# Second gated network's fills cut into pieces and its successor's loads moved, with three stages' last norm and sum on VectorE

## The chip, the cores and the metric

The program runs on one core of one Trainium2 chip. Its engines are TensorE (PE, matmuls), VectorE (DVE), ScalarE (ACT), GpSimd (POOL) and SyncE (SP, which here only issues DMAs); each has an instruction stream of its own, and they wait for one another through semaphores. The metric is the device time of one execution in microseconds (us); lower is better.

## What is computed

The reference takes x of shape (8, 512, 256) in float32 and adds to it, four times, a layer-normed sublayer of the layer-normed x:

```python
x = x + _layernorm(_L0_attn_ref(_layernorm(x)))   # differential attention, 16 heads
x = x + _layernorm(_L0_ffn_ref(_layernorm(x)))    # 2 x (window attention, gated network), each with its own residual
x = x + _layernorm(_L1_attn_ref(_layernorm(x)))   # token diffusion (16 heads), then channel diffusion
x = x + _layernorm(_L1_ffn_ref(_layernorm(x)))    # 8 experts, the best 2 of each token
# the gated network, in _L0_ffn_ref's _layer:
h = shift_token(x)                                # half the channels one token later
h = (h - mu) / sqrt(var + 1e-05) * lg + lb
a, g = split(h @ w1 + b1)                         # 682 channels each
x = x + (a * gelu(g)) @ w2 + b2
```

`_layernorm` subtracts the mean of the 256 channels and divides by sqrt(variance + 1e-5).

## The kernel before, in words

The work is a chain of seven stages, built by `build`: differential attention (names a_), window attention and gated network of layer 0 (w_, f_), the same two of layer 1, diffusion attention (c_), and the mixture of experts (d_). Both layers' tiles carry the same names in the profile, so w_ and f_ stand for two stages each; the first gated network runs from about 1690 to 1948 us of the span, the second from about 2480 to 2775. A stage reads its input from DRAM and writes its output there, in 8 batches (b = 0 to 7) of 512 tokens. A batch is one tile [128 partitions, 4 token tiles, 256 channels], 1024 numbers a partition. At its end a stage closes with a barrier of all engines (`Stage.close`, L37 to L39).

A stage's neighbour is given to it as `following`. While a stage still works, it already does the next one's first steps: `ahead_sync` issues the next stage's first loads on SP, `ahead_fill` writes its constant tiles on POOL, `ahead_gpsimd` takes its first roots on POOL (in diffusion also the norm of its input), and `ahead_vector` takes its first statistics on DVE (in diffusion also the set-up of scales and of the doubled weight wqk). The last batch's result is written to a tile of the next stage, `handed`, so that it can be stored while that stage begins; `arrived` counts that store.

*The gated network* (`gated_ffn`, L1503 on) takes each batch as follows. SP loads the shifted input (`load`, L1571 to L1574) and the residual y_res; DVE takes its statistics (`take_stats`), POOL takes the inverse root (`roots_in.step`, L102 and L104: add eps, raise to -1/2), and DVE normalises (`norm_input`, four tensor_scalar, L112) into hn. PE transposes hn (L1699), ACT brings it back as hT, PE multiplies with w1 in six chunks (L1710, L1716), ACT takes the gelu, DVE the product (`multiply`, L1786), and PE multiplies with w2 into ps_y (L1735). The order on DVE is written out: after the product of chunk 0 the statistics of the batch before's output (second network only), after chunk 1 `take_stats` of the next batch, after chunk 3 `norm_input` of the next batch, after chunk 4 the bias added to y_res (L1816), and after all chunks the sum with ps_y (`add_output`), which gives `y_taken`. PE runs one chunk ahead of DVE's products by two PSUM buffers.

In the second network (`LAST`, layer 1) the output is also normed and added to x: DVE writes the sum to yn (L1795), and POOL does `norm_output` of batch b - 1 in batch b: the root, four tensor_scalar (L1668), then one tensor_tensor with x_res (L1673); SP stores it in the next turn of its loop (L1626) and then loads the next x_res (L1646). SP's loop stands in this order: load of batch b + 1, `clear` (first network only: 4128 KB of zeros for the experts' lists, L1634), the store of batch b - 1 (second network), the wait for `y_taken` of batch b, the store of batch b (first network), and y_res of b + 1.

Where the steps of the next stage stand before the change: `ahead_sync` behind SP's loop; `ahead_fill` on POOL in batch 5 (`b + 3 == B`), a memset of packed_qk's rows 64 to 95 for all 16 heads at once (L1983), one of ones (L1985), one of v (L1986) and two small ones; `ahead_vector` on DVE in batch 7 behind chunk 2; `ahead_gpsimd` on POOL behind its loop, followed by `norm_output` of batch 7. DVE's `take_stats` and `norm_input` of batch b + 1 wait for SP's load and POOL's root; memsets stand on POOL right behind that root.

*Differential attention* (`differential_attention`, L120 on) goes by 16 steps a batch; the tail of batch b - 1 is spread over the steps of batch b, and for the last batch over a `drain` in which nothing else runs. In it: step 10 and 11 the output's statistics on DVE, step 11 POOL's root, step 12 DVE's norm (y) and POOL's `add_residual` (L393, x_res += y), step 14 DVE's `sum_stats` and POOL's root, step 15 POOL's `norm_sum` (L386), which SP stores (`store_normed`, L326) as the input of window attention.

*Diffusion attention* (`diffusion_attention`, L1831 on) ends its last batch in `drain` too: DVE's last statistics (L2682, L2687), POOL's root (L102, L104), POOL's four tensor_scalar (L2184) and its sum (L2189) into the experts' `handed`; the stage's barrier follows.

## Time and profile before

| | us |
|---|---|
| median of 3 runs | 4137.27 (4133.03 to 4146.78) |
| the profiled execution, its own time | 4133.88 |
| its span | 4132.2 |
| PE busy in the span | 3681.5 (89%) |
| DVE busy | 2371.7 (57%) |
| ACT busy | 1791.8 (43%) |
| POOL busy | 1668.0 (40%) |

A row of a timeline gives the start, the duration, the engine, the line of the kernel, the operation, the tile written and those read, the size, how many instructions are merged in the row, and in square brackets how long the engine stood idle before it and what ended that. A row that begins with a line number gives, for a tile or a line, the count, the shortest, median and longest duration in ns, and the first and last start. SPq rows are the issuing of a DMA, not its transfer. The clock of a window is the granted TensorE clock as a share of 2.4 GHz.

### The profile page before, as it was taken

The numbers are of one execution on the slowest core, as the hardware profiler recorded it, in microseconds if no ns is written. First come the engines' busy times: TensorE is split into PE (matmuls) and PEld (weight loads), VectorE is DVE, ScalarE is ACT, GpSimd is POOL, SyncE is SP. The second block draws the span as 40 slices with busy tenths as digits, with TensorE's granted clock in tenths as the row PEclk, the third lists the DMA queues.
The fourth block names the chain that finished last, engine by engine and source line by source line (L and its number), as shares of the span: only waits on it lengthen the run. The fifth ranks groups of instructions, "written<-read, shape, count | busy, mean of one in ns | idle before, by whom it ended". The sixth has DMA issues, their size and how long they took to land. (4 is left out here: it accounts for less than half of the span.)

```text
span 4132.2 us, 60613 instructions
## 1 busy us (share of the span) xinstructions
PE 3681.5 (89%) x17520; PEld 2213.3 (54%) x17520; DVE 2371.7 (57%) x6484; ACT 1791.8 (43%) x4090; POOL 1668.0 (40%) x1891
## 2 busy tenths in 40 slices
PE   6999999999869999899899989868999999758995
PEld 3556555665535555555455555533555555445664
DVE  6676777677556564233566633425666666354556
ACT  2445454454425555211455542114555555303444
POOL 2343334343356665100676642431222221165664
PEclk8999999999889999999999999988999999958997
DMA  6655665566211111345011121122222222038993
GB/s 104 73 74 68 93 83 78 66 94 80 54 54 36 41 51 38 143 179 205 16 51 51 36 74 56 54 68 74 67 59 58 68 58 53 19 135 288 318 304 133
DMA packets 223891, 377.22 MB, mean 91 GB/s; under 512 B 39180, under 2 KB 155344, under 8 KB 217264
## 3 DMA queue, kind: packets, MB, share of 16 engines
q1 hardware_dynamic: 207776, 350.99, 36.0%
q0 software_dynamic: 6480, 17.77, 1.1%
q10 hardware_dynamic: 9408, 5.78, 0.5%
q8 instruction: 100, 1.64, 0.2%
q14 instruction: 127, 1.04, 0.1%
HBM read 169.64 MB, written 84.74 MB: 62 GB/s over the span
## 5 line engine op out<-in xcount | busy, mean ns | idle before, releaser
L758 DVE CUSTOM_DVE_ANT_0 a_ps<-a_ps,a_mask 128x128 f32<-128x128 f32 (+3 forms) x1024 | 479.6, 513 | 196.7 <-PE a_ps L513 179.0
L368 POOL TENSOR_SCALAR_AFFINE_SELECT a_probs_c<-a_probs_c 128x256 f32<-128x256 f32 (+1 forms) x384 | 187.3, 504 | 668.7 <-ACT a_probs_c L663 668.3
L2505 ACT ACTIVATE c_probsT<-c_ps 128x512 f32<-128x512 f32 x512 | 298.6, 601 | 327.6 <-PE c_ps L2327 318.4
L2644 DVE TENSOR_REDUCE c_neg_max<-c_ps 128x1 f32<-128x512 f32 x512 | 337.0, 683 | 151.1 <-PE c_ps L2315 149.7
L663 ACT ACTIVATE a_probs_c<-a_ps 128x512 f32<-128x512 f32 x640 | 344.9, 603 | 99.9 <-PE a_ps L531 70.7
L513 PE MATMUL a_ps<-a_packed_qk 65*128 65x128 f32 (+3 forms) x1024 | 339.4, 375 | 46.0 <-DVE a_maxima L758 26.9
L1101 POOL TENSOR_TENSOR w_probs<-w_probs,w_inv 128x1024 f32<-128x1024 f32 x128 | 242.3, 1893 | 334.6 <-DVE w_inv L1465 334.6
L549 PE MATMUL a_ps<-a_probs_c,a_v 128*64 128x512 f32 (+3 forms) x2048 | 318.6, 455 | 0.9 <-POOL a_probs_c L368 0.8
L531 PE MATMUL a_ps<-a_packed_qk 67*128 67x512 f32 (+3 forms) x1024 | 288.6, 345 | 2.2 <-DMA a_packed_qk<-a_max_half 2.1
L1356 ACT ACTIVATE w_probs<-w_ps_s,w_neg_max 128x256 f32<-128x256 f32 x512 | 235.9, 478 | 66.8 <-DVE w_neg_max L1460 66.1
L2315 PE MATMUL c_ps<-c_packed_qk 68*128 68x512 f32 x512 | 254.7, 503 | 11.2 <-DVE c_neg_max L2644 6.6
L1164 PE MATMUL w_ps_e<-w_wqk,w_hT 128*128 128x512 f32 x512 | 247.3, 608 | 14.5 <-ACT w_hT L1306 8.0
L513 PEld LDWEIGHTS a_ps<-a_packed_qk 65*128 65x128 f32 x1024 | 186.9, 195 | 110.3 <-DVE a_maxima L758 61.1
L1460 DVE TENSOR_REDUCE w_neg_max<-w_ps_s 128x4 f32<-128x1024 f32 x128 | 155.9, 1218 | 150.1 <-PE w_ps_s L1219 150.1
L2327 PE MATMUL c_ps<-c_packed_qk 70*128 70x512 f32 x512 | 214.5, 421 | 11.8 <-ACT c_probsT L2505 8.8
L1091 POOL TENSOR_TENSOR w_inv_norm<-w_inv_norm,w_neg_half 128x8 f32<-128x8 f32 x128 | 215.5, 1683 | 10.7
L531 PEld LDWEIGHTS a_ps<-a_packed_qk 67*128 67x128 f32 x1024 | 187.8, 192 | 58.3 <-issue 43.8
L549 PEld LDWEIGHTS a_ps<-a_probs_c,a_v 128*64 128x64 f32 x2048 | 131.4, 141 | 160.0 <-issue 145.0
L1762 ACT ACTIVATE f_gelu<-f_ps_g,f_b 128x512 f32<-128x512 f32 x80 | 55.0, 687 | 346.7 <-PE f_ps_g L1716 343.9
L671 ACT COPY a_sumsT<-a_ps 128x512 f32<-128x512 f32 x128 | 74.9, 585 | 236.9 <-PE a_ps L549 236.8
L1232 PE MATMUL w_ps_x<-ident,w_probs 128*128 128x128 f32 x896 | 148.7, 283 | 28.7 <-ACT w_probsT L1345 17.4
L102 POOL TENSOR_SCALAR c_rstd<-c_mv 128x4 f32<-128x4 f32 x16 | 3.7, 230 | 421.5 <-DVE c_mv L2687 421.5
(355 smaller groups left out, 8052.1 us busy)
## 6 DMA issues: line engine op xcount, KB each, us to landing
a_packed_qk<-a_halves SPq DMA_DIRECT2D x512, 128.0 KB, 4.6
d_w<-in_L_ffn_second SPq DMA_DIRECT2D x71, 516.0 KB, 4.9
d_w<-in_L_ffn_first SPq DMA_DIRECT2D x71, 512.0 KB, 5.5
rows_dram<-f_zeros SPq DMA_DIRECT2D x8, 4128.0 KB, 16.1
c_packed_qk<-c_halves SPq DMA_DIRECT2D x256, 128.0 KB, 2.3
w_v<-w_v_next SPq DMA_DIRECT2D x16, 1024.0 KB, 4.7
d_rows<-rows_dram SPq DMA_DIRECT2D x71, 129.0 KB, 4.8
f_y_res<-y_dram SPq DMA_DIRECT2D x16, 512.0 KB, 3.9
```

The costliest lines, as they stand in the source:

```text
L513: last = nc.tensor.matmul(out[:, n * keys:(n + 1) * keys], packed_qk[0:K_ALL + 1, 0, slot, m, i * P:(i + 1) * P], packed_qk[0:K_ALL + 1, 1 ...
L531: last = nc.tensor.matmul(ps_again[u % 3][:, at:at + cols], packed_qk[0:K_ALL + 3, 1, slot, m, c * P:(c + 1) * P], packed_qk[0:K_ALL + 3, ...
L549: last = nc.tensor.matmul(ps_o[64 * m:64 * (m + 1), c * P:N], v[:, c, hd, :], probs_of(hd, k)[:, at:at + N - c * P], start=c == 0, stop=c ...
L663: nc.scalar.activation(probs_of(hd, k), ps_again[u % 3][:, :], ACT.Exp, scale=DH ** -0.5)\
L758: last = nc.vector.tensor_tensor_reduce(tile, tile, mask[:, (NT - 1 - i) * P:], 1.0, -3e38, ALU.add, ALU.max, accum_out=maxima_of[:, hd // ...
L1091: nc.gpsimd.tensor_tensor(inv_norm[:, n, :], inv_norm[:, n, :], neg_half[:, :], ALU.pow)\
L1101: nc.gpsimd.tensor_tensor(rows, rows, inv[:, s % SETS, :].unsqueeze(2).to_broadcast([P, 4, W]), ALU.mult).then_inc(weights_ready.sem, 1)
L1164: last = nc.tensor.matmul(out, hT[:, k, t * P:(t + 1) * P], right, start=k == 0, stop=k == KD - 1)
L1356: last = nc.scalar.activation(probs[:, s % SETS, r, i, :], ps_s[s % 2][:, r, i * W:(i + 1) * W], ACT.Exp, bias=neg_max[:, s % SETS, at:at ...
L2315: nc.tensor.matmul(bank("s", s)[:, :], packed_qk[0:K_ALL, 0, hd, i * P:(i + 1) * P], packed_qk[0:K_ALL, 1, hd, :], start=True, stop=True). ...
L2505: nc.scalar.activation(probsT[:, q % 2, r, :], ps_again[u % 2][:, :], ACT.Exp).then_inc(exp_done.sem, 1)
L2644: nc.vector.tensor_reduce(neg_max[:, g % 2, 0, s % GS:s % GS + 1], bank("s", s)[:, :], AX.X, ALU.max, negate=True).then_inc(max_ready.sem, 1)
```

## The change

The second network's `ahead_fill` is cut into six parts, given to batches 0 to 5: each fills packed_qk's rows for two or three heads, one memset a head, and the last part also does the rest, v by token tile. `ahead_sync` moves from behind SP's loop into batch 5 (`b == B - 3`), behind `clear` and ahead of the store and the wait for `y_taken`; that holds for both gated networks. `ahead_vector` moves from batch 7 to batch 6. In the last batch of differential attention the residual's sum and the norm of the sum, in that of the second gated network and of diffusion the output's norm and sum, go from POOL to DVE; POOL keeps the roots. The other batches stay as they are.

```diff
--- before.py
+++ after.py
@@ -25,7 +25,7 @@
         self.nc, self.name, self.side = nc, name, side
         self.ctx = ExitStack()
         self.ctx.semaphores = []
-        self.ahead_sync = self.ahead_vector = self.ahead_gpsimd = self.ahead_fill = lambda eng: None
+        self.ahead_sync = self.ahead_vector = self.ahead_gpsimd = self.ahead_fill = lambda eng, part=0: None
 
     def sb(self, name, shape, dt=fp32):
         return self.ctx.enter_context(self.nc.sbuf_tensor(self.name + name, shape, dt, side=self.side))
@@ -407,11 +407,11 @@
                         norm_heads(ref(b, d), j)
                 if s in (9, 10) and 1 in live:
                     norm_input(ref(b, 1), (2 * (s - 9), 2 * (s - 9) + 1))
-                if s == 12 and -1 in live:
+                if s == 12 and -1 in live and 0 in live:
                     add_residual(ref(b, -1))
                 if s == 14 and -1 in live:
                     roots_sum.step(pool, ref(b, -1), 0, rstd_y[:, :], mv_y[:, :, 1], EPS, neg_half[:, :, 0])
-                if s == 15 and -1 in live:
+                if s == 15 and -1 in live and 0 in live:
                     norm_sum(ref(b, -1))
                 if s == 11 and -1 in live:
                     roots_y.step(pool, ref(b, -1), 0, rstd_y[:, :], mv_y[:, :, 1], EPS, neg_half[:, :, 0])
@@ -821,6 +821,18 @@
                 last = normalise(nc, y[:, t, :], y[:, t, :], mv_y, rstd_y, t)
                 if t == NT - 1:
                     last.then_inc(y_normed.sem, 1)
+
+
+            def add_last(b):
+                dve.wait_ge(res_loaded.sem, res_loaded.at(b, 16))
+                dve.wait_ge(y_normed.sem, y_normed.at(b, 1))
+                nc.vector.tensor_tensor(x_res[:, :, :], x_res[:, :, :], y[:, :, :], ALU.add).then_inc(y_ready.sem, 1)
+
+            def norm_last(b):
+                roots_sum.wait(dve, b, 0)
+                for t in range(NT):
+                    last = normalise(nc, y[:, t, :], x_res[:, t, :], mv_y, rstd_y, t)
+                last.then_inc(normed_ready.sem, 1)
 
             def extras(b, uses, live):
                 for kind, n, d in uses:
@@ -857,9 +869,13 @@
                         if s == 12:
                             for t in range(NT):
                                 norm_output(ref(b, -1), t)
+                            if 0 not in live:
+                                add_last(ref(b, -1))
                         if s == 14:
                             for t in range(NT):
                                 sum_stats(ref(b, -1), t)
+                            if 0 not in live:
+                                norm_last(ref(b, -1))
                 extras(b, END.get(s, ()), live)
 
             def set_up():
@@ -1641,6 +1657,8 @@
                     sp.wait_ge(hn_ready.sem, hn_ready.at(b, 1))
                     load(sp, b + 1)
                 clear(b)
+                if b == B - 3:
+                    following.ahead_sync(sp)
                 if LAST and b >= 1:
                     store(b - 1)
                     sp.dma_start(x_res[:, :, :], x_v[b]).then_inc(x_res_in.sem, 16)
@@ -1651,7 +1669,6 @@
                     sp.dma_start(y_res[:, :, :], y_v[b + 1]).then_inc(y_res_in.sem, 16)
             if cleared is not None:
                 sp.dma_start(cleared[B * B * N:, :], zeros[:, 0:D + 2]).then_inc(zeros_out.sem, 16)
-            following.ahead_sync(sp)
             store(B - 1)
             if cleared is not None:
                 sp.wait_ge(zeros_out.sem, 16 * (B + 1))
@@ -1661,32 +1678,31 @@
             def norm_output(b):
                 roots.step(pool, b, 0, rstd_y[:, :], mv_y[:, :, 1], EPS, neg_half[:, :])
                 pool.wait_ge(roots.ready.sem, roots.ready.at(b, 1))
-                out = following.handed if b == B - 1 else out_sb
                 if b >= 1:
                     pool.wait_ge(stored.sem, stored.at(b - 1, 16))
                 for t in range(NT):
-                    last = nc.gpsimd.tensor_scalar(out[:, t, :], yn[:, t, :], mv_y[:, t, 0:1], rstd_y[:, t:t + 1],
+                    last = nc.gpsimd.tensor_scalar(out_sb[:, t, :], yn[:, t, :], mv_y[:, t, 0:1], rstd_y[:, t:t + 1],
                                                    ALU.subtract, ALU.mult)
                 last.then_inc(normed.sem, 1)
                 pool.wait_ge(normed.sem, normed.at(b, 1))
                 pool.wait_ge(x_res_in.sem, x_res_in.at(b, 16))
-                nc.gpsimd.tensor_tensor(out[:, :, :], out[:, :, :], x_res[:, :, :], ALU.add).then_inc(y_ready.sem, 1)
+                nc.gpsimd.tensor_tensor(out_sb[:, :, :], out_sb[:, :, :], x_res[:, :, :], ALU.add).then_inc(y_ready.sem, 1)
 
             for b in range(B):
                 if LAST and b >= 1:
                     norm_output(b - 1)
                 if b + 1 < B:
                     roots_in.step(pool, b + 1, 0, rstd[:, :], mv[:, :, 1], EPS, neg_half[:, :])
-                if b + 3 == B:
-                    if LAST:
+                if b < B - 2:
+                    if LAST and b >= 1:
                         pool.wait_ge(y_ready.sem, y_ready.at(b - 1, 1))
                     pool.wait_ge(roots_in.ready.sem, roots_in.ready.at(b + 1, 1))
-                    following.ahead_fill(pool)
+                    following.ahead_fill(pool, b)
             if LAST:
                 pool.wait_ge(y_ready.sem, y_ready.at(B - 2, 1))
             following.ahead_gpsimd(pool)
             if LAST:
-                norm_output(B - 1)
+                roots.step(pool, B - 1, 0, rstd_y[:, :], mv_y[:, :, 1], EPS, neg_half[:, :])
 
         @block.tensor
         def _(pe):
@@ -1816,11 +1832,22 @@
                         nc.vector.tensor_tensor(y_res[:, :, :], y_res[:, :, :],
                                                 b2[:, :].unsqueeze(1).to_broadcast([P, NT, D]), ALU.add)\
                           .then_inc(biased.sem, 1)
-                    if c == 2 and b + 1 == B:
+                    if c == 2 and b + 2 == B:
                         following.ahead_vector(dve)
                 add_output(b)
+            def norm_last(b):
+                roots.wait(dve, b, 0)
+                out = following.handed
+                for t in range(NT):
+                    last = normalise(nc, out[:, t, :], yn[:, t, :], mv_y, rstd_y, t)
+                last.then_inc(normed.sem, 1)
+                dve.wait_ge(normed.sem, normed.at(b, 1))
+                dve.wait_ge(x_res_in.sem, x_res_in.at(b, 16))
+                nc.vector.tensor_tensor(out[:, :, :], out[:, :, :], x_res[:, :, :], ALU.add).then_inc(y_ready.sem, 1)
+
             if LAST:
                 output_stats(B - 1)
+                norm_last(B - 1)
 
         own.close()
 
@@ -1919,6 +1946,7 @@
     x_loaded, stats_linked, in_order = signal("x_loaded", 16), signal("stats_linked"), signal("in_order", 5)
     hn_ready, kept, hT_psum = signal("hn_ready"), signal("kept"), signal("hT_psum", KD)
     passed_pool, passed_dve = signal("passed_pool", 0), signal("passed_dve", 0)
+    filled = signal("filled")
     roots_in = InverseRoots(ctx, nc, "c_roots_in", 1)
 
     first = []
@@ -1979,13 +2007,21 @@
                                            ALU.subtract, ALU.mult)
         last.then_inc(hn_ready.sem, 1)
 
-    def ahead_fill(pool):
-        nc.gpsimd.memset(packed_qk[2 * ROWS:3 * ROWS, :, :, :].bitcast(fp32), 1.0).then_inc(made_pool.sem, 1)
-        pool.wait_ge(made_pool.sem, 1)
-        nc.gpsimd.memset(ones[:, :], 1.0)
-        nc.gpsimd.memset(v[:, :, :, :], 0.0).then_inc(made_pool.sem, 1)
-        pool.wait_ge(made_pool.sem, 2)
-        nc.gpsimd.memset(v[:, :, :, DH:DH + 1], 1.0)
+
+    FILLS = 6
+
+    def ahead_fill(pool, part):
+        heads = range(part * H // FILLS, (part + 1) * H // FILLS)
+        for hd in heads:
+            nc.gpsimd.memset(packed_qk[2 * ROWS:3 * ROWS, :, hd, :].bitcast(fp32), 1.0).then_inc(filled.sem, 1)
+        pool.wait_ge(filled.sem, (part + 1) * H // FILLS)
+        if part < FILLS - 1:
+            return
+        nc.gpsimd.memset(ones[:, :], 1.0).then_inc(made_pool.sem, 1)
+        for t in range(NT):
+            nc.gpsimd.memset(v[:, t, :, :], 0.0).then_inc(filled.sem, 1)
+        pool.wait_ge(filled.sem, H + NT)
+        nc.gpsimd.memset(v[:, :, :, DH:DH + 1], 1.0).then_inc(made_pool.sem, 1)
         nc.gpsimd.memset(neg_half[:, :], -0.5).then_inc(made_pool.sem, 1)
         pool.wait_ge(made_pool.sem, 3)
 
@@ -2185,8 +2221,7 @@
                                                    ALU.subtract, ALU.mult)
                 last.then_inc(y_normed.sem, 1)
                 standing_wait(pool, y_normed.sem, y_normed.at(b, 1), passed_pool.sem)
-                out = following.handed if isinstance(b, int) and b == B - 1 else x_res
-                nc.gpsimd.tensor_tensor(out[:, :, :], x_res[:, :, :], y[:, :, :], ALU.add).then_inc(y_ready.sem, 1)
+                nc.gpsimd.tensor_tensor(x_res[:, :, :], x_res[:, :, :], y[:, :, :], ALU.add).then_inc(y_ready.sem, 1)
 
             def body(b, live):
                 if -1 in live:
@@ -2204,7 +2239,8 @@
                 make_h(b - 1)
                 root_between(b - 1)
                 following.ahead_gpsimd(pool)
-                norm_output(b - 1)
+                roots.step(pool, b - 1, 1, rstd[:, :], mv[:, :, 1], EPS, neg_half[:, :])
+                standing_wait(pool, roots.ready.sem, roots.ready.at(b - 1, 2), passed_pool.sem)
 
             batches(pool, lambda: None, body, drain)
 
@@ -2773,11 +2809,20 @@
                 for s in range(STEPS):
                     step(b, s, live)
 
+            def norm_last(b):
+                roots.wait(dve, b, 1)
+                for t in range(NT):
+                    last = normalise(nc, y[:, t, :], h[:, t, :], mv, rstd, t)
+                last.then_inc(y_normed.sem, 1)
+                dve.wait_ge(y_normed.sem, y_normed.at(b, 1))
+                nc.vector.tensor_tensor(following.handed[:, :, :], x_res[:, :, :], y[:, :, :], ALU.add).then_inc(y_ready.sem, 1)
+
             def drain(b):
                 for s in range(STEPS):
                     step(b, s, (-1,))
                     if s == GS * G // 2 + GS // 4:
                         following.ahead_vector(dve)
+                norm_last(b - 1)
 
             batches(dve, before, body, drain)
 
```

## Rows read from the trace of the kernel before

**Rows 1.** The page's first line.

```profile
span 4132.2 us, 60613 instructions
```

**Rows 2.** Windows of core 0; columns after the stretch: length, busy time and count by engine, clock.

```profile
2727.00:2746.00 19.00, 3.18 (x8) 1.14 (x6) 2.79 (x12) 0.69 (x1) 7.42 (x11) 0.68 0.51 152
2761.40:2775.00 13.60, 0.00 (x0) 0.00 (x0) 3.01 (x9) 0.00 (x0) 8.44 (x7) 0.62 0.04 14
2775.00:2790.00 15.00, 9.38 (x16) 3.92 (x16) 1.41 (x2) 4.51 (x8) 0.31 (x2) 0.66 0.28 72
```

**Rows 3.** DVE sums of batches 4, 5, 6, 7 of the second gated network.

```profile
L1795 DVE TENSOR_TENSOR f_yn<-f_y_res,f_ps_y x1: 1222/1222/1222, 2635.8 to 2635.8; 128x1024 f32<-128x1024 f32 x1
...
2682.34 1.22 DVE L1795 TENSOR_TENSOR f_yn<-f_y_res,f_ps_y 128x1024 f32<-128x1024 f32 x1 [10.96 <-PE f_ps_y L1735]
...
2712.86 1.22 DVE L1795 TENSOR_TENSOR f_yn<-f_y_res,f_ps_y 128x1024 f32<-128x1024 f32 x1 [9.91 <-PE f_ps_y L1735]
...
2761.41 1.22 DVE L1795 TENSOR_TENSOR f_yn<-f_y_res,f_ps_y 128x1024 f32<-128x1024 f32 x1 [9.28 <-PE f_ps_y L1735]
```

**Rows 4.** The fill on POOL, and DVE's normalising beside it, batch 5.

```profile
2652.51 13.74 POOL L1983 MEMSET c_packed_qk<- 32x16384 f32 x1
...
L112 DVE TENSOR_SCALAR f_hn<-f_shifted,f_mv,f_rstd x4: 396/1182/13979, 2652.4 to 2668.5; 128x256 f32<-128x256 f32 x4
```

**Rows 5.** The same normalising in batch 6, the product before it, PE's next transposes.

```profile
2696.33 0.75 DVE L1786 SCALAR_TENSOR_TENSOR f_gated<-f_ps_a,f_b,f_gelu 128x512 f32<-128x512 f32 x1 [1.87 <-issue]
2699.01 1.38 DVE L112 TENSOR_SCALAR f_hn<-f_shifted,f_mv,f_rstd 128x256 f32<-128x256 f32 x4 [1.93 <-POOL f_rstd L104]
...
2701.22 1.04 PE L1699 MATMUL f_ps_t<-ident,f_hn 128*128 128x128 f32 x8
```

**Rows 6.** DVE in batch 7: statistics and set-up for the next stage.

```profile
2736.71 1.41 DVE L1999 BATCH_NORM_STATS2 c_stats_in<-c_x_in 128x6 f32<-128x256 f32 x4 [12.55 <-DMA c_x_in<-x_dram]
...
2744.98 0.36 DVE L2014 TENSOR_SCALAR c_q_scale<-c_q_scale 128x4 f32<-128x4 f32 x1 [6.34 <-DMA c_neg_norm<-in_con_neg_norm]
```

**Rows 7.** SP's issues in the second gated network.

```profile
2638.52 0.34 SPq L1574 DMA_DIRECT2D f_shifted<-y_dram  x1
...
2731.56 0.51 SPq L1950 DMA_DIRECT2D c_x_in<-x_dram  x1
...
2745.76 0.43 SPq L1955 DMA_DIRECT2D c_block_mask<-in_con_block_mask  x1
```

**Rows 8.** SP's issues in the first gated network.

```profile
1858.33 2.93 SPq L1634 DMA_DIRECT2D rows_dram<-f_zeros  x1
...
1885.23 0.40 SPq L1626 DMA_DIRECT2D y_dram<-f_out  x1
...
1921.63 1.62 SPq L971 DMA_DIRECT2D w_x_in<-y_dram  x1
...
1925.96 4.64 SPq L973 DMA_DIRECT2D w_scale<-in_L_ffn_q_scale  x1
...
1933.94 0.91 SPq L973 DMA_DIRECT2D w_crossed_scale<-in_L_ffn_k_scale  x2
```

**Rows 9.** POOL's last norms and sums in three stages, and a sum on DVE.

```profile
1145.42 2.34 POOL L393 TENSOR_TENSOR a_x_res<-a_x_res,a_y 128x1024 f32<-128x1024 f32 x1 [1.60 <-DVE a_y L112]
...
1151.47 4.84 POOL L386 TENSOR_SCALAR a_y<-a_x_res,a_mv_y,a_rstd_y 128x256 f32<-128x256 f32 x4 [0.22 <-POOL a_rstd_y L104]
...
2766.25 4.83 POOL L1668 TENSOR_SCALAR c_handed<-f_yn,f_mv_y,f_rstd_y 128x256 f32<-128x256 f32 x4
2771.16 2.34 POOL L1673 TENSOR_TENSOR c_handed<-c_handed,f_x_res 128x1024 f32<-128x1024 f32 x1
...
3613.69 4.84 POOL L2184 TENSOR_SCALAR c_handed<-c_h,c_mv,c_rstd 128x256 f32<-128x256 f32 x4 [0.22 <-POOL c_rstd L104]
3618.71 2.34 POOL L2189 TENSOR_TENSOR d_handed<-c_x_res,c_handed 128x1024 f32<-128x1024 f32 x1 [0.18 <-POOL c_handed L2184]
...
2700.97 1.22 DVE L1816 TENSOR_TENSOR f_y_res<-f_y_res,f_b 128x1024 f32<-128x1024 f32 x1
```

## Prediction, before the run

> **What bounds the kernel now.** The page's first line gives the span, 4132.2 us [rows 1]. The program is a chain of seven stages on one core, each closed by a barrier of all engines, so time can be won inside a stage only where its own last wait gets shorter, and at its end only where the chain up to the barrier does. I read the windows by stretch first, for holes in TensorE (PE) in the second gated network and around its end. In the window at 2727 PE works 3.18 of 19 us; in the one at 2761.4 it works none of 13.6 [rows 2].
>
> Then I took the DVE sum that closes each batch of that stage, as a clock [rows 3]: batches 4 and 5 are 46.5 us apart, 5 and 6 are 30.5, 6 and 7 are 48.5. PE works without a break in the middle interval, so 30.5 is PE's own pace and the other two each hold a stall. The reader is to see what each stall is.
>
> Batch 5's: POOL fills 16 heads of the next stage's packed_qk in one memset of 13.74 us, and the four normalisations of hn on DVE, 1.38 us together in batch 6 [rows 5], last up to 13.98 us each beside it [rows 4]. PE needs hn for its next transposes. An instruction on DVE waits for one on POOL here without any semaphore between them.
>
> Batch 7's: DVE stands 12.55 us before the statistics of c_x_in and 6.34 us before c_q_scale, both for DMAs [rows 6]. SP issues those loads only from 2731.56 to 2746.19, after the loop's last batch [rows 7]; the products that PE waits for are queued behind DVE's waits.
>
> **The change, part by part.** *Fills in pieces.* The one fill becomes 16 of one head, in batches 0 to 5 (2, 3, 3, 2, 3, 3 of them), each set right behind the root that DVE's normalisation also waits for. Removed: batch 5's stall, 46.5 - 30.5 = 16.0 us. Put back: a piece takes 13.74/16 = 0.86 us, 0.93 with some start (estimate). In rows 4 the longest normalisation, begun at 2652.4, ends at 2666.4, 0.2 us behind the fill (2652.51 + 13.74), so DVE gets in when a fill ends, though more fills are queued. I count one normalisation let through behind each piece: with three pieces the fourth ends some 3.3 us after the start instead of 1.38, 1.9 late. PE has cover: hn ends at 2700.39 and the transposes start at 2701.22, when PE is done with earlier products, 0.8 us later [rows 5]. Left 1.1 us per batch of three pieces, 0.4 per batch of two. In batch 0 POOL has no output norm ahead of its root and DVE comes later than the pieces (0). Batches 1 to 5: 4 x 1.1 + 0.4 = 4.8 us. Bounds: 0 if DVE always gets in first; 16 x 0.93 less 6 x 0.8 is 10.1, with some 2 us for the rest of batch 5's fills 12. I take 4.8, since the one boundary in rows 4 shows DVE getting in.
> The Trainium skill (SBUF — State Buffer, Who interferes with whom) says that DVE in its two-port modes and POOL lock the shared port pair against each other for whole instructions, and whoever issues first has it. By that rule a waiting normalisation goes before a memset queued later, which is the count above; a memset that always wins would give the upper bound. The trace agrees with the full block (13.98 us), and has one boundary between pieces.
>
> *Loads sooner.* The next stage's loads go to SP's place in batch 5, behind load(6) (its last issue at 2638.52) and ahead of the store of batch 4, the load of x_res and the wait for y_taken. 28 issues take 14.6 us [rows 7], 0.5 each, so SP is through at about 2653.5; what is queued behind them (that store, x_res for POOL's sum a batch later) has slack, and y_taken of batch 5 comes only after about 2666 in the new time. Cost 0; without that cover, up to 14.6 us. In the first gated network the same move puts 13.2 us of issues (1921.63 to 1934.85) behind a clear issued by 1861.26, and SP's next store is at 1885.23: 24.0 us of room [rows 8]. There the loads held nothing up before either, so gain 0, cost 0.
>
> *Set-up on DVE one batch sooner.* With the loads landed, batch 7 keeps its PE pace: 30.5 less about 0.9 for transposes that have no successor (1.04 in rows 5), 29.6. Gain 48.5 - 29.6 = 18.9 us. The work itself, some 2.9 us (1.41 of statistics, then aggregation, three small ones and a copy), now goes into batch 6 behind the third product. The fourth product began at 2696.33 and the normalisation after it waited for POOL until 2699.01 [rows 5]: 2.7 us of room, with 0.8 behind it. Cost 0, bounds 0 and 2.9. POOL's ahead_gpsimd then runs early in batch 7 and is done before its last root.
>
> *Last norm and sum on DVE, three times.* On POOL four normalisations are 4.84 us and a sum of 128x1024 is 2.34 [rows 9]; on DVE 1.38 [rows 5] and 1.22 (same shape, two SBUF inputs) [rows 9]. In the second gated network POOL's pair goes from 2766.25 to 2773.50, 7.25 us; DVE's is 1.38 + 0.1 + 1.22 = 2.7: gain 4.6. In diffusion 3613.69 to 3621.05 gives 4.7. In differential attention the sum gains 1.2 with its handover and the norm 3.5: 4.7. All stand on the chain to the barrier, POOL has nothing beside them, and SP stores after them. Sum 14.0; bounds 0 (SP or a landing sets the barrier) and 15.
>
> **Sum**: 16.0 - 4.8 + 18.9 + 14.0 = 44.1 us. The profiled execution took 4133.88 us (1.7 outside the span): 4089.8. The median of the three runs is 4137.27, 3.4 above it: 4093.2. I predict the middle, 4091.5.
>
> **Rivals.**
> (a) *The lock holds through all pieces*: 12 us put back, not 4.8: 4099. For it: POOL's pieces are queued without a wait between them. Against: rows 4's boundary.
> (b) *Pieces free, or the clock held.* If DVE gets in first: 4087. The granted clock was 0.62 over the 13.6 us hole before diffusion and 0.66 in the 15 us after it, PE working 9.38 us there [rows 2]; at full clock that would be about half. The hole shrinks to 9 us; were the clock kept, up to 4.7 us go too: 4087, both together 4082. The Trainium skill (TensorE: Matmul & The Clock Gate, Part 1) says that an idle TensorE falls back to 1.2 GHz; by it a hole of 9 us is still idle enough and the sum stays. No row shows a hole of that length here.
> (c) *The change doesn't deliver a part.* Set-up waits in batch 6 as it did in batch 7: 18.9 us lost, 4110. For it: SP's queue now carries these loads beside the batch's own. Against: 39 us from first issue to use, against 14.4 before (2731.56 to 2746). Or the barriers wait for SP's landings and the 14.0 are lost: 4105.5.
> (d) *Slower.* SP becomes the bound in batch 5 of the second gated network. One load of this kind took 4.64 us to issue [rows 8]; 28 at that pace are 130 us against 27.5 before y_taken, so y_res and batch 7's load come 102 us late and the forecast becomes 4193.5. It decides from about 2.5 us an issue on: 28 x 2.5 - 27.5 = 42.5 us, the whole way from 4091.5 back to the profiled 4133.9. Against: the same issues took 0.5 us each in rows 7.
>
> **How the numbers follow.** Forecast 0.58, (a) 0.12, (b) 0.13, (c) 0.13, (d) 0.02; 0.02 is for what I haven't seen. The range goes down to (b)'s near-best, 4083, and up to (c)'s second form, 4106; about 0.15 lies outside. A measurement can tell about 0.3% from no change, 12.4 us: all but (d), and a pile-up of (a) and both forms of (c), are faster by more than that. Faster 0.95, same 0.03, slower 0.02.
>
> **What would show it.** The DVE sums of the second gated network 31.6 us apart over batches with three pieces and 30.9 over the one with two (30.5 if pieces are free, 32.5 for three by (a)), then 30.5 and 29.6; normalisations of up to 0.9 us beside memsets of 0.9; no DVE wait for c_x_in; SP's loads at 0.5 us each behind load(6) of batch 5; next stages starting 4.6 to 4.7 us sooner after each last statistics. Wrong would be a stall of 10 us or more in batch 6, SP late for y_taken, or a barrier that doesn't move with DVE's sum.

## The result and the profile after

The changed kernel took 4104.42 us, the median of 5 runs (4091.46 to 4112.28). The kernel before, run beside it, took 4146.78 (5 runs, 4133.03 to 4156.11; three of them are the runs of the table in "Time and profile before"). The ratio is 0.9904, its 95% interval 0.9877 to 0.9931: about 1% faster, and beyond what a measurement can tell from no change. The time lies inside the predicted range (4083 to 4106), 12.9 us above the predicted 4091.5.

The profiled execution of the changed kernel took 4112.28 us, the slowest of its five, against 4133.88 for the profiled one of before. So this pair of traces differs by 21.6 us only, while the medians differ by 42.4. The page's first line of the changed kernel:

```profile
span 4110.6 us, 60567 instructions
```

**The second gated network's clock.** The DVE sum that closes each batch of that network, timeline of DVE in the changed kernel; compare [rows 3]:

```profile
2516.76 1.22 DVE L1811 TENSOR_TENSOR f_yn<-f_y_res,f_ps_y 128x1024 f32<-128x1024 f32 x1 [9.91 <-PE f_ps_y L1751]
...
2549.16 1.22 DVE L1811 TENSOR_TENSOR f_yn<-f_y_res,f_ps_y 128x1024 f32<-128x1024 f32 x1 [9.29 <-PE f_ps_y L1751]
...
2581.16 1.22 DVE L1811 TENSOR_TENSOR f_yn<-f_y_res,f_ps_y 128x1024 f32<-128x1024 f32 x1 [9.29 <-PE f_ps_y L1751]
...
2612.45 1.22 DVE L1811 TENSOR_TENSOR f_yn<-f_y_res,f_ps_y 128x1024 f32<-128x1024 f32 x1 [9.29 <-PE f_ps_y L1751]
...
2644.45 1.22 DVE L1811 TENSOR_TENSOR f_yn<-f_y_res,f_ps_y 128x1024 f32<-128x1024 f32 x1 [9.29 <-PE f_ps_y L1751]
...
2676.45 1.22 DVE L1811 TENSOR_TENSOR f_yn<-f_y_res,f_ps_y 128x1024 f32<-128x1024 f32 x1 [9.29 <-PE f_ps_y L1751]
...
2707.02 1.22 DVE L1811 TENSOR_TENSOR f_yn<-f_y_res,f_ps_y 128x1024 f32<-128x1024 f32 x1 [9.29 <-PE f_ps_y L1751]
...
2736.66 1.22 DVE L1811 TENSOR_TENSOR f_yn<-f_y_res,f_ps_y 128x1024 f32<-128x1024 f32 x1 [9.03 <-PE f_ps_y L1751]
```

Intervals, from batches 0 to 1 up to 6 to 7: 32.4, 32.0, 31.3, 32.0, 32.0, 30.6, 29.6 us. Before they were 30.5 four times, then 46.6, 30.5 and 48.5. Both stalls are gone, and five batches have become 0.8 to 1.9 us longer.

**Why they are longer.** Batch 2's root and memsets on POOL, DVE's normalising, and PE's next transposes, one fence for each engine of the changed kernel; compare [rows 4, 5]:

```profile
2564.77 1.04 POOL L104 TENSOR_TENSOR f_rstd<-f_rstd,f_neg_half 128x4 f32<-128x4 f32 x1
2565.93 3.02 POOL L2016 MEMSET c_packed_qk<- 32x1024 f32 x3
```

```profile
2565.84 3.57 DVE L112 TENSOR_SCALAR f_hn<-f_shifted,f_mv,f_rstd 128x256 f32<-128x256 f32 x4 [1.95 <-POOL f_rstd L104]
```

```profile
2569.47 1.09 PE L1715 MATMUL f_ps_t<-ident,f_hn 128*128 128x128 f32 x8 [1.28 <-DVE f_hn L112]
```

The four normalisations take 3.57 us where they took 1.38 in [rows 5]; they end at 2569.41, and PE, idle for 1.28 us, starts its transposes 0.06 later. This is the small form of the block in [rows 4].

**The set-up in batch 6.** DVE in the changed kernel, from the next stage's statistics to the normalising; compare [rows 6]:

```profile
2688.13 1.40 DVE L2035 BATCH_NORM_STATS2 c_stats_in<-c_x_in 128x6 f32<-128x256 f32 x4
2689.68 0.38 DVE L2042 BATCH_NORM_AGGREGATE c_mv_in<-c_stats_in 128x2 f32<-128x6 f32 x4
2689.97 1.82 DVE L2050 TENSOR_SCALAR c_q_scale<-c_q_scale 128x4 f32<-128x4 f32 x1
2691.71 0.21 DVE L2051 TENSOR_SCALAR c_n_sign<-c_tau_n,c_rows 16x2 f32<-16x2 f32 x1
2691.84 0.21 DVE L2052 TENSOR_SCALAR c_n_take<-c_tau_n,c_rows 16x2 f32<-16x2 f32 x1
2691.97 0.67 DVE L2053 COPY c_wqk<-c_wqk_in 128x1024 f32<-128x1024 f32 x1
2692.68 0.75 DVE L1802 SCALAR_TENSOR_TENSOR f_gated<-f_ps_a,f_b,f_gelu 128x512 f32<-128x512 f32 x1
2693.90 1.38 DVE L112 TENSOR_SCALAR f_hn<-f_shifted,f_mv,f_rstd 128x256 f32<-128x256 f32 x4 [0.47 <-POOL f_rstd L104]
```

No wait for a DMA is left. POOL beside it, from its sum for the batch before to the root that the normalising waits for:

```profile
2689.42 2.35 POOL L1689 TENSOR_TENSOR f_out<-f_out,f_x_res 128x1024 f32<-128x1024 f32 x1
2691.74 1.00 POOL L102 TENSOR_SCALAR f_rstd<-f_mv 128x4 f32<-128x4 f32 x1
```

The two engines held each other up. c_q_scale took 1.82 us where it took 0.36 in [rows 6], and ended at 2691.80, 0.03 behind POOL's sum. Then POOL's first step of the root took 1.00 us, where the same step took 0.23 in batch 2, and ended at 2692.74, 0.10 behind DVE's copy. So the normalising came late by 0.8 us: 17.45 behind the sum of batch 5, against 16.67 in [rows 3, 5]. It ended at 2695.28, and PE started its transposes at 2695.34, still on time, with nothing to spare.

**SP.** Issues around the moved loads; compare [rows 7]:

```profile
2647.22 0.34 SPq L1590 DMA_DIRECT2D f_shifted<-y_dram  x1
2647.60 3.60 SPq L1978 DMA_DIRECT2D c_x_in<-x_dram  x1
...
2664.98 0.43 SPq L1983 DMA_DIRECT2D c_block_mask<-in_con_block_mask  x1
2665.45 0.43 SPq L1642 DMA_DIRECT2D x_dram<-f_out  x1
...
2677.70 0.37 SPq L1669 DMA_DIRECT2D f_y_res<-y_dram  x1
```

They go from 2647.60 to 2665.41, 17.8 us, with 3.60 for the first one alone. The store behind them leaves at 2665.45, the load of x_res is issued by 2669.92, and y_res, whose wait ends with `y_taken` of batch 5, at 2677.70, right after the sum at 2676.45.

**The ends of three stages.** The first PE instruction behind the barriers of differential attention, the second gated network and diffusion, with PE's idle time ahead of it in brackets. Before:

```profile
1160.83 1.94 PE L1156 MATMUL w_ps_e<-ident,w_x_in 128*128 128x128 f32 x8 [19.95 <-PEq L39]
...
2775.14 1.94 PE L2267 MATMUL c_ps<-ident,c_hn 128*128 128x128 f32 x8 [13.77 <-PEq L39]
...
3623.11 1.94 PE L3090 MATMUL d_ps_z<-ident,d_h 128*128 128x128 f32 x8 [13.75 <-PEq L39]
```

After:

```profile
1163.65 1.94 PE L1172 MATMUL w_ps_e<-ident,w_x_in 128*128 128x128 f32 x8 [15.14 <-PEq L39]
...
2745.68 1.94 PE L2303 MATMUL c_ps<-ident,c_hn 128*128 128x128 f32 x8 [9.06 <-PEq L39]
...
3591.75 1.94 PE L3135 MATMUL d_ps_z<-ident,d_h 128*128 128x128 f32 x8 [8.53 <-PEq L39]
```

The idle times fall from 19.95 to 15.14, from 13.77 to 9.06 and from 13.75 to 8.53 us: 4.8, 4.7 and 5.2. They hardly scatter: over the profiles of all kernels below they are 19.9 to 20.0, 13.7 to 13.8 and 13.5 to 13.8 us with the norm and sum on POOL, and 15.1, 9.1 to 9.4 and 8.5 to 8.6 with both on DVE. The work that now stands in the second of them, DVE of the changed kernel; compare [rows 9]:

```profile
2741.43 1.38 DVE L112 TENSOR_SCALAR c_handed<-f_yn,f_mv_y,f_rstd_y 128x256 f32<-128x256 f32 x4 [1.59 <-POOL f_rstd_y L104]
2742.85 1.22 DVE L1846 TENSOR_TENSOR c_handed<-c_handed,f_x_res 128x1024 f32<-128x1024 f32 x1
```

**By stage.** Lengths from the first PE instruction behind one barrier to that behind the next (the last one to the end of the span), in us. "Tails" is the norm and sum on DVE. The two means are over profiled executions of the kernels below, without the tails and with them:

| stage | before | after | after, second profile | mean of 5 without tails | mean of 8 with tails |
|---|---|---|---|---|---|
| differential attention | 1160.8 | 1163.7 | 1151.6 | 1161.2 | 1154.9 |
| first gated network | 258.1 | 258.2 | 258.0 | | |
| second gated network | 296.4 | 264.1 | 264.0 | | |
| diffusion | 848.0 | 846.1 | 841.5 | 848.5 | 843.8 |
| experts | 509.1 | 518.8 | 513.5 | 513.2 | 514.6 |

The second gated network is 32.3 and 32.4 us shorter in the two profiles. In the first profile of the changed kernel differential attention and the experts are 12 and 5 us longer than in its second, with the same code; and the experts of the kernel before took 513.3 us in its own second profile. So the stages scatter from one execution to the next by as much as parts of the change are worth, and in the first pair of traces this hid half of the gain.

### The profile page after: what moved, and what is told of

Same layout as the page of the kernel before. It is cut to its first block and busy times, and to the rows that moved or that the text cites. A ratio compares the mean times of both kernels' runs of the same rounds, so it can differ in the third digit from the quotient of the medians.

```text
span 4110.6 us, 60567 instructions
## 1 busy us (share of the span) xinstructions
PE 3683.6 (90%) x17456; PEld 2210.7 (54%) x17520; DVE 2374.8 (58%) x6499; ACT 1793.7 (44%) x4090; POOL 1652.7 (40%) x1894
## 5 line engine op out<-in xcount | busy, mean ns | idle before, releaser
L1107 POOL TENSOR_TENSOR w_inv_norm<-w_inv_norm,w_neg_half 128x8 f32<-128x8 f32 x128 | 215.2, 1681 | 10.7
```

The source lines that it names most:

```text
L1107: nc.gpsimd.tensor_tensor(inv_norm[:, n, :], inv_norm[:, n, :], neg_half[:, :], ALU.pow)\
```

## Experiments

Each run's time stands against the kernel before, run on the same chip at the same time. The first four share 27 runs of it, median 4140.71; the next four 11 runs, median 4139.79; the last three 11 runs, median 4134.89.

### The whole change again, and each of its parts alone

*The whole change again* is the changed kernel with no edit.

> The changed kernel once more, nothing altered. In its first profile the second gated network is 32.3 us shorter than before, but the body of differential attention (up to PE's last work on the last batch) is 8.6 us longer and the mixture of experts 9.8 us longer (518.9 against 509.1), and neither holds work that the change touches there. Theory (scatter): those two are differences from run to run, so in this profile both move freely, by several us, while the second gated network keeps 264.1 within 0.5; the span is around 4132.2 - 41.7 = 4090.5 where both are short. Rival (real cost): the change makes both stages slower, through code or data placed otherwise; then differential attention and experts are again 8 to 10 us longer, and the span is within 3 us of 4110.

4095.32 us, ratio 0.9898 (0.9873 to 0.9923).

*Fills alone:* the kernel before, with the new `ahead_fill` and POOL's part of the loop.

```diff
-                if b + 3 == B:
+                if b < B - 2:
...
-                    following.ahead_fill(pool)
+                    following.ahead_fill(pool, b)
```

> The kernel before with the fills alone cut in pieces over batches 0 to 5. Theory (terms add up): the second gated network is 296.4 - 16.0 + 7.2 = 287.6 us long, with sums of DVE 32 us apart over three pieces and 31.3 over two, and the 48.5 us of batch 7 kept; 8.8 us faster. Rival (the lock costs more than the pieces show, or the pieces were free and the 1.5 us came from the moved loads): 291 or more, or 30.5 us apart and 280.4 in all.

4131.46 us, ratio 0.9979 (0.9963 to 0.9995). The network took 288.7 us, 7.7 less than before and 1.1 more than expected; batches 0 to 5 show the same intervals as in the whole change. The interval up to the sum of batch 7, with its wait for DMAs, was 50.2 us here. It scatters: in the five profiles that keep this stall it is 48 to 50 us.

*Loads and set-up alone:*

```diff
                 clear(b)
+                if b == B - 3:
+                    following.ahead_sync(sp)
...
-            following.ahead_sync(sp)
...
-                    if c == 2 and b + 1 == B:
+                    if c == 2 and b + 2 == B:
                         following.ahead_vector(dve)
```

> The kernel before with ahead_sync in batch 5 and ahead_vector in batch 6 alone; one fill in batch 5. Theory: batch 7 goes from 48.5 to 29.6 us, batches 1 to 4 keep 30.5, batch 5 its 46.5: second gated network 277.5 us, 18.9 us faster, and the first gated network keeps its 258.1. Rival (the loads cost elsewhere): SP's issues, which took 17.8 us instead of 14.6 behind load(6), or a batch 6 above 31 us give part of it back: 280 us or more, or the first gated network 2 us or more longer.

4123.1 us, ratio 0.9954 (0.9937 to 0.9971). The network took 277.5 us, 18.9 less; the last intervals are 30.5 and 29.6, and batch 5's stays at 46.6. The first gated network took 261.6 us, 3.4 more than in the first profile of before, which the expectation had as a sign that the loads cost something there. They don't explain it: the kernel before, without the move, took 260.8 there in its second profile, and the changed kernel, with it, 258.2 and 258.0.

*Tails alone:* the changed kernel with fills, loads and set-up put back where they were.

> The kernel before with the last batch's norm and sum on DVE in three stages alone. Theory: three chains to a barrier get 4.7, 4.6 and 4.7 us shorter: 14.0 us faster, second gated network 291.8 us. Rival (landings or the clock take it): the barrier comes only when SP's store has landed or TensorE starts colder, so less than 8 us in all, and the gap from DVE's last instruction to the next stage's first on PE grows by what the engine saved.

4130.0 us, ratio 0.9978 (0.9962 to 0.9995). The network took 292.3 us, 4.1 less.

In their stage the three parts give 7.7, 18.9 and 4.1, together 30.7 of the whole's 32.3; the 1.6 left is no more than the scatter of batch 7's interval. By medians they give 9.2, 17.6 and 10.7, together 37.5 against 45.4 for the whole; the four intervals are some 7 to 10 us wide to either side, so that gap says nothing.

### The kernel before again

No edit.

> The kernel before once more, for its stages. Over five profiles differential attention has been 1151.6 to 1163.7 us long, diffusion 840.2 to 851.8 and the experts 509.1 to 518.9, in no order of what the change has in them. Theory (scatter): the kernel before shows the same spread, so at least one of the three differs from its first profile by 3 us or more, while its second gated network is 296.4 within 0.5. Rival: these stages are steady in one kernel (1160.8, 848.0 and 509.1 within 1) and the experts' extra 4 to 10 us come from the change.

4139.07 us, with 1160.3, 845.3 and 513.3 us in differential attention, diffusion and the experts, and 297.1 in the second gated network, 0.7 more than in the first profile. The experts are 4.3 us longer than in the first profile of the same kernel, so the rival has nothing left to stand on. It adds one to the profiles without the tails in the table above.

### How DVE and the memsets share: smaller and larger pieces

*Half pieces:* two memsets a head.

```diff
         for hd in heads:
-            nc.gpsimd.memset(packed_qk[2 * ROWS:3 * ROWS, :, hd, :].bitcast(fp32), 1.0).then_inc(filled.sem, 1)
+            for side_of in range(2):
+                last = nc.gpsimd.memset(packed_qk[2 * ROWS:3 * ROWS, side_of, hd, :].bitcast(fp32), 1.0)
+            last.then_inc(filled.sem, 1)
```

> The changed kernel with each head's fill as two memsets of 32x512 instead of one of 32x1024. Theory (DVE gets one normalisation in behind each memset): the fourth normalisation waits for four halves instead of three wholes and ends some 2.3 us after the start instead of 3.57; batches 1 to 5 come down from 32.0 and 31.3 us to 30.6 to 31.0, and the second gated network from 264.0 to about 259. Rival (DVE waits until POOL's queue of fills is empty, whatever the pieces): the four take 3.5 us or more again and the batches keep 32.0 and 31.3, or grow with the start-up of the added memsets.

4093.1 us, ratio 0.9893 (0.987 to 0.9916); the network 259.8 us. The intervals of batches 1 to 5 are 31.4, 31.0, 31.0, 31.0 and 31.0: the batch with two heads, four memsets now, costs as much as those with three heads and six, since only four normalisations are there to be held up. DVE in batch 2 of this kernel, with 2.59 us where 2.3 were expected:

```profile
2549.22 2.59 DVE L112 TENSOR_SCALAR f_hn<-f_shifted,f_mv,f_rstd 128x256 f32<-128x256 f32 x4 [1.93 <-POOL f_rstd L104]
```

*One memset a part*, over its two or three heads together:

```diff
-        for hd in heads:
-            nc.gpsimd.memset(packed_qk[2 * ROWS:3 * ROWS, :, hd, :].bitcast(fp32), 1.0).then_inc(filled.sem, 1)
-        pool.wait_ge(filled.sem, (part + 1) * H // FILLS)
+        nc.gpsimd.memset(packed_qk[2 * ROWS:3 * ROWS, :, heads[0]:heads[-1] + 1, :].bitcast(fp32), 1.0).then_inc(filled.sem, 1)
+        pool.wait_ge(filled.sem, part + 1)
```

> The changed kernel with the two or three heads of a part in one memset. Theory (DVE in behind each memset): the first normalisation waits 2.6 us, the other three are free; four take 3.7 to 3.9 us against 3.57, so batches of three heads go to 32.1 to 32.4 us, of two to 31.3 or so: nearly no difference, since three normalisations already waited for the three pieces. Rival (the cost is in the number of memsets): clearly shorter than 32.0.

4107.94 us in one run; the network 269.4 us. DVE and then POOL in its batch 2:

```profile
2559.60 3.85 DVE L112 TENSOR_SCALAR f_hn<-f_shifted,f_mv,f_rstd 128x256 f32<-128x256 f32 x4 [1.92 <-POOL f_rstd L104]
```

```profile
2559.68 2.65 POOL L2015 MEMSET c_packed_qk<- 32x3072 f32 x1
```

Four normalisations take 2.59 us beside memsets of 32x512, 3.57 beside 32x1024, and 3.85 beside a single one of 32x3072. One normalisation gets through behind each memset, so shorter memsets cost less. With one memset the block is that memset (2.65 us): the first normalisation takes 2.88 us, the other three 0.40 each.

The intervals of this kernel hold a surprise: 34.3, 32.3, 31.4, 32.3 and 34.5, so two batches with three heads are 2 us longer than two others with as many. PE in its batches 1 and 2, transposes and the products behind them:

```profile
2529.57 1.09 PE L1715 MATMUL f_ps_t<-ident,f_hn 128*128 128x128 f32 x8 [1.92 <-DVE f_hn L112]
2530.49 12.41 PE L1751 MATMUL f_ps_y<-f_w,f_gated 128*128 128x256 f32 x48
```

```profile
2563.50 1.09 PE L1715 MATMUL f_ps_t<-ident,f_hn 128*128 128x128 f32 x8 [1.52 <-DVE f_hn L112]
2564.43 10.72 PE L1751 MATMUL f_ps_y<-f_w,f_gated 128*128 128x256 f32 x48
```

The same 48 matmuls took 12.41 us in batch 1 and 10.72 in batch 2. The windows of this kernel over the two (columns as in [rows 2]):

```profile
2530.50:2542.80 12.30, 12.30 (x50) 10.02 (x48) 1.46 (x2) 1.27 (x2) 0.00 (x0) 0.86 0.02 5
2564.40:2575.00 10.60, 10.60 (x50) 8.87 (x48) 1.49 (x2) 1.30 (x2) 0.00 (x0) 1.00 0.01 2
```

In batch 1 PE had been idle for 1.92 us, and the granted clock over the following 12.3 us was 0.86, a mean over the clock's two levels, 1.00 and 0.50; in batch 2 it had been idle for 1.52 us, and the clock stayed at 1.00. Before batch 5's transposes PE was idle for 2.09 us, since there the first fills of v stand behind the one memset and held up two more normalisations (0.69 us each); its 48 matmuls took 12.20 us, and that interval is the other long one.

### Memsets queued behind the normalisation

The changed kernel, where POOL waits for hn before each part:

```diff
                     pool.wait_ge(roots_in.ready.sem, roots_in.ready.at(b + 1, 1))
+                    pool.wait_ge(hn_ready.sem, hn_ready.at(b + 1, 1))
                     following.ahead_fill(pool, b)
```

> The changed kernel with one wait more on POOL: each part of the fills waits until DVE has normalised hn of the next batch, so that nothing is to be normalised beside it; POOL has some 19 us idle there. Theory (all of the 7.2 us that batches 1 to 5 lose are the lock on the normalisations): they come down to 30.5 us, the second gated network to 264.0 - 7.2 = 256.8, and the kernel is 49 us faster than before. Rival (the bias sum with two SBUF inputs, the product or the sum with PSUM wait for the fills too): only part of it comes back, 259 or more, and one of those DVE rows is longer than its 1.22 or 0.75 us.

4094.86 us, ratio 0.9896 (0.9876 to 0.9915); the network 256.8 us. All intervals of batches 1 to 5 are 30.5. The changed kernel had taken 4095.32 us at another time, so this says nothing yet of the 7 us between their networks; both were run again side by side:

> The changed kernel once more, beside the one with its fills behind the normalisation. Theory (the second gated network is 32.3 us shorter and the rest of the program only scatters): median between 4092 and 4106 us, stage of the second gated network 264 us, like 264.07 and 264.01 in its two profiles so far. Rival (the first 4104.4 us was the change's true time and something outside the network pays for it): median above 4102 and the first stage and the diffusion longer than in the profiles of the kernel before (1160.8 and 848.0; 1160.3 and 845.3).

> The changed kernel with each memset queued behind the normalisation, once more, on the same chip as the changed kernel. Theory (the 7.2 us taken off the network reach the end): median 3 to 10 us below the changed kernel's of this call, stage of the network 256.8 us. Rival (something takes them back behind the network): medians within 2 us and a later stage longer by as much in this profile and in the one before.

The changed kernel took 4100.51 us, ratio 0.9919 (0.9904 to 0.9935), with memsets behind 4092.21, ratio 0.9896 (0.9881 to 0.991): 8.3 us less. The two intervals still touch; the networks, 264.3 and 256.3 us, show where the difference is. DVE and then POOL in batch 2 of the kernel with the memsets behind:

```profile
2558.90 1.38 DVE L112 TENSOR_SCALAR f_hn<-f_shifted,f_mv,f_rstd 128x256 f32<-128x256 f32 x4 [1.92 <-POOL f_rstd L104]
2560.86 1.22 DVE L1833 TENSOR_TENSOR f_y_res<-f_y_res,f_b 128x1024 f32<-128x1024 f32 x1
```

```profile
2560.43 2.73 POOL L2017 MEMSET c_packed_qk<- 32x1024 f32 x3 [1.56 <-DVE f_hn L112]
```

The normalising is back at 1.38 us. The sum that adds the bias, begun at 2560.86 amid the memsets, takes the 1.22 us of [rows 9]: an addition of two SBUF tiles is not blocked by them.

*The one large fill of before, behind the normalisation:* the same line in the kernel before, nothing else.

> The kernel before with its one fill of batch 5's buffer queued behind the first normalisations, nothing else changed. Theory (what costs is the memset beside the normalisation, not its size): the stage of the network 296.4 - 16.1 = 280.3 us, batch 4 to 5 at 30.5 us, and some 4124 us in one look. Rival (the memset is late for its scatter now, and the products wait for it): batch 4 to 5 above 32 us.

4127.24 us in one run; the network 280.2 us, batches 4 to 5 30.5 apart. POOL and then DVE of this kernel in batch 5:

```profile
2657.92 13.74 POOL L1984 MEMSET c_packed_qk<- 32x16384 f32 x1 [1.56 <-DVE f_hn L112]
```

```profile
2656.39 1.38 DVE L112 TENSOR_SCALAR f_hn<-f_shifted,f_mv,f_rstd 128x256 f32<-128x256 f32 x4 [1.94 <-POOL f_rstd L104]
2657.69 0.74 DVE L1787 SCALAR_TENSOR_TENSOR f_gated<-f_ps_a,f_b,f_gelu 128x512 f32<-128x512 f32 x1
2658.35 1.22 DVE L1817 TENSOR_TENSOR f_y_res<-f_y_res,f_b 128x1024 f32<-128x1024 f32 x1
```

The memset is as long as ever, 13.74 us, and costs nothing in this stage: POOL had 20.4 us here between two roots (2656.36 to 2676.81). One line takes the whole 16.1 us stall away; cutting the fill into 16 pieces took away 16.1 and put 7.2 back.

## Why the prediction came out as it did

Two steps failed: the base that the sum was taken from, and the term for what the fills put back, 4.8 us, which was 7.2.

**The base.** The prediction put its sum against 4135.6, the middle of one profiled execution (4133.88) and the median of three runs (4137.27). Beside the changed kernel the one before had a median of 4146.78, over the same three runs and two more, 4154.94 and 4156.11. Of the 12.9 us that the forecast was too low, 11.2 are this base (4146.78 - 4135.6), and 1.7 the gain (44.1 predicted, 42.4 between the medians). How the miss divides is chance too. Over the three times that both kernels ran side by side the changed one had a mean of 4100.1 us, 8.6 above the forecast: 5.2 from the base (mean 4140.8) and 3.4 from the gain (40.7 in the mean). The kernel before had medians of 4146.78, 4140.71, 4139.79 and 4134.89 at four times, and single runs from 4122.7 to 4156.1; three runs do not fix such a base to 5 us, and the range was narrow for it: its lower and upper ends took in the terms of the change but nothing for the base.

**Stall of batch 5, 16.0 removed:** right. It was 16.1, shown by the one fill queued behind the normalisation.

**Fills, 4.8 put back:** this term was mis-sized; it was 7.2. The mechanism, one normalisation let through behind each memset, held and is shown by the sizes 32x512, 32x1024 and 32x3072. The terms were off: beside the normalising a memset takes 1.0 us, not 0.93 (3.02 for three; 2.73 when nothing is between them), so four normalisations end after 3.57 us and not 3.3. PE's cover was 0.7, not 0.8 (2.19 us later, 1.5 of interval longer). So batches 2, 4 and 5 cost 1.5 each, not 1.1, and batch 3 0.8, not 0.4. Batch 1 cost 1.9, since PE's cover is shorter there, and that stood in the trace of before. DVE of the kernel before, the normalising in batches 1 and 2:

```profile
2530.77 1.38 DVE L112 TENSOR_SCALAR f_hn<-f_shifted,f_mv,f_rstd 128x256 f32<-128x256 f32 x4 [2.32 <-POOL f_rstd L104]
...
2560.90 1.38 DVE L112 TENSOR_SCALAR f_hn<-f_shifted,f_mv,f_rstd 128x256 f32<-128x256 f32 x4 [1.94 <-POOL f_rstd L104]
```

In batch 1 it begins 17.06 us behind the sum of batch 0 (2513.71), in batch 2 16.68 behind that of batch 1 (2544.22), while PE's transposes come 18.88 behind in both: 0.4 us of cover in place of 0.8. The prediction read its cover in one batch and used it for five. Its evidence for one normalisation behind each piece was thin as well: at the boundary in [rows 4] POOL itself waited (0.06 us, `pool.wait_ge(made_pool.sem, 1)`) before the next memset, which the queued pieces don't do. That the count held was shown only afterwards. Rival (a), all pieces block (12 us), and the free pieces of (b) are both out: that the 7.2 us were this block is shown by their full return once the memsets stand behind.

Memset and normalising wait for the same root; DVE's first one is recorded 0.09 us ahead of the memset (2565.84 against 2565.93), as in [rows 4], and is held up all the same. The Trainium skill (SBUF — State Buffer, Who interferes with whom) says that whoever issues first holds the shared pair. With a waiting normalisation ahead of each later memset the traces agree, by 2.59, 3.57 and 3.85 us for three sizes; for the first pair the recorded starts speak against it, if they are the times of issue, which no run here tells.

**Loads sooner and set-up in batch 6, 18.9:** right in the sum; the loads and set-up alone shortened the network by 18.9 us. But the prediction costed the set-up, 2.9 us, as if DVE were alone, and left out that DVE and POOL hold each other up there too. It lasted 4.5 us (2688.13 to 2692.68), and POOL's root came 0.8 us late. Its 2.7 us of room were misread too: DVE stood idle for 1.87 us before the fourth product and for 1.93 behind it [rows 5], 3.8 in all. In the kernel with the loads and set-up alone the same two instructions took 1.88 and 1.0 us; that DVE's copy is what held POOL's root is argued from these times. PE's cover took all of it and was used up, so that it cost nothing was luck. SP's issues took 17.8 us, not 14.6; 12.3 were left before y_res. Rival (c), the set-up waits again, and (d), SP as the bound, are out: from 2.5 us an issue (d) would have decided, and it was 0.6.

**Tails, 14.0:** right. The idle times at the three barriers fell by 14.7 in the profile, so SP's landings do not set the barriers, the second form of (c). Over 13 profiled executions differential attention is 6.3 and diffusion 4.7 us shorter with them; with 4.7 in the network that is 15.7, as near as stages that scatter by 5 to 12 us can show it.

**The clock behind the shorter hole:** as the forecast had it, and against (b): it does not stay up. The windows of the changed kernel over the start of diffusion (columns as in [rows 2]):

```profile
2746.00:2755.00 9.00, 5.40 (x12) 2.39 (x10) 0.83 (x2) 3.30 (x5) 0.32 (x2) 0.50 0.06 21
2755.00:2770.00 15.00, 10.07 (x24) 4.17 (x24) 4.01 (x7) 3.02 (x5) 0.00 (x0) 0.57 0.31 71
```

After 9.06 us without work for PE the granted clock is 0.50 over the first 9 us, the lower of its two levels (1.2 of 2.4 GHz), and 0.57 over the next 15. Over the first 15 us of diffusion it was 0.50 here and 0.67 in the kernel before, but the hole's length does not make that difference: with the loads alone, behind a hole of 13.74 us, it was 0.50, and with half pieces, behind 9.06 us, 0.68. What makes it is open.

**The sum**, with the measured sizes: 16.1 - 7.2 + 18.9 + 14.7 = 42.5 us, against 44.1 predicted, and 42.4, 45.4 and 34.4 between the medians at three times. It is faster, the case given 0.95. That the time of 4104.42 fell inside the range, near its upper end, is no merit of the sum: the range held nothing for the base, which made most of the miss.

## What to carry to other kernels

A POOL memset and a DVE tensor_scalar set loose by the same event collide; queue the filler behind the work that PE waits for, and it may then fill the time that POOL has idle there (13.74 us of 20.4 here). Cutting it up only cuts the price, and leaves one piece per DVE instruction to pay. Read a cover in every batch that is to use it. And a base taken from three runs is a term of the sum like any other: give it a width, and check a pair of traces stage by stage before reading their difference as the change.

## What the runs showed of the hardware

**A short idle time can cost more than itself.** In the kernel with one memset a part, 1.92 us without work for PE were followed by a granted clock of 0.86, and 48 matmuls took 1.7 us more; 1.52 us were followed by no such drop. So a normalising that lasted some 0.3 us longer than in the changed kernel (3.85 against 3.57 in batch 2) made batch 1's interval 1.9 us longer. Idle time alone does not decide: in the first gated network of the same kernel PE was once idle for 2.13 us, and the clock stayed at 1.00 over the 15 us from there.

**The stages' scatter comes with the clock.** The same 5568 matmuls of PE in the first 1150 us, windows of the changed kernel in its first and then in its second profile:

```profile
0.00:1150.00 1150.00, 1051.08 (x5568) 648.90 (x5568) 780.83 (x3103) 534.08 (x1042) 421.49 (x565) 0.96 0.57 78
```

```profile
0.00:1150.00 1150.00, 1042.55 (x5568) 645.82 (x5568) 785.85 (x3120) 532.96 (x1042) 422.71 (x569) 0.97 0.58 79
```

PE was busy for 8.5 us more in the first, at a clock of 0.96 against 0.97, and that stage was 12.1 us longer. What moved the clock there was not tried.

**DVE and POOL hold each other up in both directions.** A DVE tensor_scalar waits for a POOL memset (13.98 us beside 13.74) and lasts until POOL's sum of two SBUF tiles ends (c_q_scale, 1.82 us for 0.36); a POOL tensor_scalar of 128x4 took 1.00 us for 0.23 beside DVE's set-up. A DVE sum of two SBUF tiles (1.22 us) and a product with one input in PSUM (0.74) kept their times beside memsets.
